# Half of a head's feature product moved ahead of the head before's attention product, with W2's splits, evictions and sums moved beside it

## Chip, cores and metric

One Trainium2 chip, one of its cores. The metric is the device time in microseconds from the kernel's start to its end.

## What is computed

A graph attention network of two layers on 512 nodes and 16,896 edges, then a residual and a layer norm. The first layer has 8 heads of 768 features, the second one head.

```
h = (x @ W).reshape(n, H, C)
alpha_s = einsum('nhc,hc->nh', h, a_s);  alpha_d = einsum('nhc,hc->nh', h, a_d)
e = leaky_relu(alpha_s[src] + alpha_d[dst], 0.2)
e = exp(e - segment_max(e, dst)[dst])
alpha = e / (segment_sum(e, dst)[dst] + 1e-16)
out = segment_sum(h[src] * alpha, dst) + b
...
h = elu(gat_layer(x, W1, ..., 8 heads, concat))
out = gat_layer(h, W2, ..., 1 head)
x = layernorm(x + out)
```

The kernel counts the edges into a dense 512 by 512 matrix and works with dense products from then on.

## The kernel before

The program is written engine by engine: each engine has its own list of instructions, in the order in which it is written out, and the engines meet at semaphores only. For each head h of the first layer there are three big products on TensorE, each in three passes of 32-bit operands split into a high and a low part (high by high, high by low, low by high):

- **B(h, n)**, n from 0 to 7 (`half_B`): x times W1 of the head. n = 2t + c is the half c (384 columns) of the row tile t (128 nodes). 18 matmuls each.
- **C(h, c)**, c from 0 to 5 (`stage_C`): the head's finished features, 128 at a time, times the rows of W2 that belong to them, summed over all heads in PSUM banks O. TensorE does C of head h-1 while the scores of head h are made.
- **A(h, c)**, c from 0 to 5 (`stage_A`): the head's rows h times its attention weights P. 12 matmuls each.

TensorE's order in head h from 3 on is: B(h, 0) to B(h, 7), C(h-1, 0), the small transposes `sources`, C(h-1, 1), the small transposes `targets`, C(h-1, 2) to C(h-1, 5) with the softmax `denominators` inside the last, A(h, 0) to A(h, 5). B, the small products and A take turns in two PSUM banks, R[0] and R[1]; the table `RING` says in which order, and `take` waits until the use two places back was released (`released`): a B by the eviction of its half, `den` by the reciprocal, an A by its scaling.

The other engines feed this. ScalarE casts the high parts of W1 and W2 out of a ring of five raw tiles Wr (`high_w1`, `high_w2`), evicts B to h32 (`evict_B`), casts h (`high_h`), and does its share of the `scores`: for each of four row tiles an Identity (L452), an Exp (L455) and the high part of P (L460). Then `high_sums` (L470) casts the column sums for the denominators. VectorE makes the sums of h with the attention vectors (`sums_h`, L717, two for a tile), in the scores the leaky maximum (L782, one input in PSUM), the product with the counts (L788, both inputs in SBUF), sums of two tiles (L793) and of all (L908), then the reciprocal of the denominators (`reciprocals`, L807), the scaling of A and the ELU. `products_W2` (L736, two for a tile) multiplies raw W2 rows of head 7 with the second layer's attention vectors; `V_OF` puts three tiles into each of two heads. GpSimd subtracts the low parts: of W1 (`low_w1`, L1060), of W2 (`low_w2`, L1066) and of P (`low_P`, L1070). SyncE issues all loads in the order of `LOADS`, each when the tile five places back has been used up.

Of the kernel before, what the change touches and what calls it, by code (L numbers as in the profile page):

```python
# [5 lines left out]
def gat_resnorm_kernel(nc, x, xT, src, dst, W1, as1, ad1, b1c, W2, as2, ad2, b2, out):  # L6
# [18 lines left out]
    EARLY = 3  # L25
# [26 lines left out]
    RING += [("r2", 2, 0), ("r1", 2, 0), ("den", 2, 0)] + [("A", 2, c) for c in range(FT)]  # L52
# [13 lines left out]
    with ctx:  # L66
# [188 lines left out]
        def sync_program(e):  # L255
# [79 lines left out]
            for h in range(EARLY, H):  # L335
                if h + 1 < H:
                    load_abc(h + 1 if h + 2 < H else H)
                for k in range(FT):
                    load_raw("w2", h - 1, k)
                if h + 2 == H:  # L340
                    load_abc(H - 1)
                if h + 1 < H:
                    for k in range(FT):
                        load_raw("w1", h + 1, k)
                for k in V_OF.get(h, ()):
# [18 lines left out]
        def scalar_program(e):  # L364
# [175 lines left out]
            for h in range(H):  # L540
# [18 lines left out]
                if h == 2:  # L559
                    high_w2(1, 4)  # L560
                    scaled_as(2, 24)
                    scores(2, 2, 0, NT, ring_bank("r2", 2, 0), (gl_value(1, FT - 1), (s_g, 2 * FT)), 8, lambda u: high_w2(1, 5) if u == 3 else None)
                    high_h(2, 0)
                    high_h(2, 1)
                    high_sums(2)
                    high_h(2, 2)
                    high_h(2, 3)
                if 0 < h < EARLY:
                    e.wait_ge(s_den, h + 1)
                    e.copy(rb[:, :], ring_bank("den", h, 0)[:, :]).then_inc(s_dc, 1)  # L570
                if h == 2:

                    e.wait_ge(s_hl, 3 * NT)
                    for k in range(3, FT):
                        high_w1(3, k)
# [864 lines left out]
```

## Time and profile before

| | us |
|---|---|
| median of 3 runs | 641.19 (640.8 to 641.33) |
| the profiled execution, its own time | 641.08 |
| its span, first to last instruction | 639.3 |
| TensorE busy | 632.1 (99% of the span) |
| VectorE busy | 518.9 (81%) |
| ScalarE busy | 337.8 (53%) |
| GpSimd busy | 204.4 (32%) |

The sum of a prediction is made against 641.08; the median of the runs is 0.11 us above it. The shares are means over stages that differ: the edge counting (the first fifth), eight heads, and the second layer from about 586 us on. The granted clock of TensorE was 0.998 in the mean.

### The profile page before, as it was taken

The page shows a single profiled execution, that of the slowest core. Times are in us where ns is not written, and L with a number is a line of the kernel's source. Part 1 is how long each engine was busy: PE and PEld are TensorE (multiplying, and loading weights), DVE is VectorE, ACT ScalarE, POOL GpSimd, SP SyncE. Part 2 cuts the span into 40 slices and gives each one's busy share as a digit, 9 for nine tenths or more (in the row PEclk, how much of TensorE's full clock was granted, in tenths as well). Part 3 has the DMA queues.
Part 4 walks back from the last instruction along what each step waited for, and adds up shares of the span by engine and source line. Part 5 has one row for each costly group of instructions (what it writes and reads, how often), then busy time and mean ns, then how long its engine had stood idle before and what let it go on. Part 6 is the DMA issues. An engine that isn't in the chain of part 4 may idle for free.

```text
span 639.3 us, 9306 instructions
## 1 busy us (share of the span) xinstructions
PE 632.1 (99%) x3426; PEld 542.7 (85%) x3426; DVE 518.9 (81%) x928; ACT 337.8 (53%) x570; POOL 204.4 (32%) x122
## 2 busy tenths in 40 slices
PE   9999999999999999999999999999999999999996
PEld 6766568989888889988898889988998899887885
DVE  8999997889989987475855685567898589889876
ACT  7899992546524754353545454463545444534382
POOL 1000000140743630357124822374136604551230
PEclk9999999999999999999999999999999999999999
DMA  8422402115154420234113330316025401800002
GB/s 313 166 75 75 154 20 99 50 54 194 51 148 140 158 74 1 60 91 148 50 51 91 97 110 25 95 45 183 26 90 159 123 26 51 293 28 1 1 2 99
DMA packets 22173, 59.36 MB, mean 93 GB/s; under 512 B 2544, under 2 KB 2800, under 8 KB 22128
## 3 DMA queue, kind: packets, MB, share of 16 engines
q1 hardware_dynamic: 21984, 58.69, 28.6%
q8 instruction: 28, 0.46, 0.3%
q14 instruction: 17, 0.14, 0.1%
q10 hardware_dynamic: 144, 0.07, 0.0%
HBM read 54.03 MB, written 4.72 MB: 92 GB/s over the span
## 4 chain that ended last, share of the span: by engine, by line
PE 82%; DVE 16%; issue 1%; DMA 0%; ACT 0%; DVEq 0%
PE O L1238 30%; PE R L1136 8%; PE R L1133 8%; PE R L1139 8%; PE R L1205 6%; PE R L1211 6%; PE R L1208 6%; DVE ohd L679 4%; DVE ohs L683 2%; PE O L1150 2%; DVE junk L717 2%; DVE junk L736 2%; PE R L1155 1%; DVE W1l L705 1%; PE O L1205 1%
## 5 line engine op out<-in xcount | busy, mean ns | idle before, releaser
L1066 POOL TENSOR_TENSOR W2l<-Wr,W2h 128x768 fp32r<-128x768 f32 x48 | 93.3, 1953 | 207.8 <-ACT W2h L411 207.8
L1070 POOL TENSOR_TENSOR Pl<-L,Ph 128x512 fp32r<-128x512 f32 x34 | 54.0, 1599 | 166.7 <-ACT Ph L460 166.4
L1133 PE MATMUL R<-W1h,xTh 128*128 128x384 f32 x312 | 105.8, 339 | 0.0
L1139 PE MATMUL R<-W1h,xTl 128*128 128x384 f32 x312 | 104.9, 336 | 0.0
L1136 PE MATMUL R<-W1l,xTh 128*128 128x384 f32 x312 | 104.8, 336 | 0.0
L717 DVE CUSTOM_DVE_ANT_0 junk<-h,abc 128x768 bf16<-128x768 f32 x64 | 62.6, 978 | 41.8 <-ACT h L423 37.4
L1238 PE MATMUL O<-W2h,gh 128*128 128x256 f32 (+1 forms) x384 | 78.6, 339 | 0.0
L1238 PE MATMUL O<-W2h,gl 128*128 128x256 f32 (+1 forms) x384 | 77.4, 336 | 0.0
L1238 PE MATMUL O<-W2l,gh 128*128 128x256 f32 (+1 forms) x384 | 77.3, 335 | 0.0
L423 ACT COPY h<-R 128x384 f32<-128x384 f32 x62 | 29.5, 477 | 73.0 <-PE R L1139 70.9
L1060 POOL TENSOR_TENSOR W1l<-Wr,W1h 128x768 fp32r<-128x768 f32 x30 | 55.4, 1868 | 37.5 <-ACT W1h L400 37.5
L1205 PE MATMUL R<-Ph,hh 128*128 128x512 f32 x168 | 66.2, 394 | 0.0
L1211 PE MATMUL R<-Ph,hl 128*128 128x512 f32 x168 | 65.9, 392 | 0.0
L1238 PEld LDWEIGHTS O<-W2l,gh 128*128 128x128 f32 x384 | 59.0, 188 | 8.0
L1238 PEld LDWEIGHTS O<-W2h,gl 128*128 128x128 f32 x384 | 59.0, 188 | 8.0
L1208 PE MATMUL R<-Pl,hh 128*128 128x512 f32 x168 | 65.2, 388 | 0.0
L1238 PEld LDWEIGHTS O<-W2h,gh 128*128 128x128 f32 x384 | 58.1, 188 | 6.5 <-issue 0.2
L1150 PE MATMUL O<-ohd,ohs 128*128 128x512 bf16 x264 | 60.3, 382 | 0.4 <-DVE ohs L683 0.4
L1133 PEld LDWEIGHTS R<-W1h,xTh 128*128 128x128 f32 x312 | 58.7, 188 | 0.7
L1136 PEld LDWEIGHTS R<-W1l,xTh 128*128 128x128 f32 x312 | 58.7, 188 | 0.4
L1139 PEld LDWEIGHTS R<-W1h,xTl 128*128 128x128 f32 x312 | 58.6, 188 | 0.0
L411 ACT CAST W2h<-Wr 128x768 fp32r<-128x768 f32 x48 | 39.5, 833 | 29.7 <-PE O L1238 22.8
(186 smaller groups left out, 1171.5 us busy)
## 6 DMA issues: line engine op xcount, KB each, us to landing
Wr<-in_W SPq DMA_DIRECT2D x101, 384.0 KB, 3.3
abc<-in_as SPq DMA_DIRECT2D x9, 384.0 KB, 4.0
abc<-in_ad SPq DMA_DIRECT2D x9, 384.0 KB, 5.9
h_rows<-h SPq DMA_DIRECT2D x8, 384.0 KB, 2.4
hl<-h_rows SPq DMA_DIRECT2D x8, 384.0 KB, 5.9
xin<-in_xT SPq DMA_DIRECT2D x6, 256.0 KB, 6.1
xr<-in_x SPq DMA_DIRECT2D x1, 1536.0 KB, 7.5
out<-res SPq DMA_DIRECT2D x4, 384.0 KB, 2.3
```

Source lines behind the costliest of these rows:

```text
L717: e.tensor_tensor_reduce(out=junk[:, :], in0=get, in1=a_ap[:, i, :], op0=ALU.mult, op1=ALU.add, scale=1.0, scalar=0.0, accum_out=asd[:, h ...
L1060: e.tensor_tensor(W1l[:, k, :], Wr[:, n, :], W1h[:, k, :].bitcast(f32), ALU.subtract).then_inc(s_w1l, 1)
L1066: e.tensor_tensor(W2l[:, m % N2, :], Wr[:, n, :], W2h[:, m % N2, :].bitcast(f32), ALU.subtract).then_inc(s_w2l, 1)
L1070: e.tensor_tensor(Pl[:, t, d0:d1], L[:, t, d0:d1], Ph[:, t, d0:d1].bitcast(f32), ALU.subtract).then_inc(s_Pl, 1)
L1133: e.matmul(bank[:, 0:HALF], xTh[:, f, xs], hi[:, ws], start=f == 0, stop=False)
L1136: e.matmul(bank[:, 0:HALF], xTh[:, f, xs], lo[:, ws], start=False, stop=False)
L1139: m = e.matmul(bank[:, 0:HALF], xTl[:, f, xs], hi[:, ws], start=False, stop=f == FT - 1)
L1150: e.matmul(O[2 * (g % 2) + q][:, :], ohs[:, r, 128 * q:128 * q + 128], ohd[:, r, :], start=j == STARTS[g], stop=j == STARTS[g + 1] - 1).th ...
L1205: e.matmul(bank[:, :], hh[:, t, cs], Ph[:, t, :], start=t == 0, stop=False)
L1208: e.matmul(bank[:, :], hh[:, t, cs], Pl[:, t, :], start=False, stop=False)
L1211: m = e.matmul(bank[:, :], hl[:, t, cs], Ph[:, t, :], start=False, stop=t == NT - 1)
L1238: mm = e.matmul(ob, ga[:, c, 128 * t:128 * t + 128], wa[:, q, lo:hi], start=first and (hi - lo == 512 or t % 2 == 0), stop=last, skip_grou ...
```

## The change

It writes the same instructions in another order; the numbers of products, casts and subtractions stay. TensorE does B(h+1, 0) to B(h+1, 3) between C(h-1, 4) and C(h-1, 5), so ahead of A(h), for h from 2 to 6; `targets` come after C(h-1, 2). For this W1 of head h+1 is cast and subtracted earlier (the last four casts between the instructions of the scores), W2's tile 5 later, and tiles 0 to 3 of the next W2 in the same head. ScalarE evicts the four early halves after `high_sums`, and B(h+1, 4) ahead of the last cast of g. VectorE does `sums_h` of the two early row tiles ahead of `reciprocals`, and in heads 5 and 6 the three `products_W2` there too.

```diff
     for h in range(EARLY, H):
-        LOADS += [("w2", h - 1, k) for k in range(FT)]
+        LOADS += [("w2", h - 1, k) for k in range(5)]
         LOADS += [("w1", h + 1, k) for k in range(FT) if h + 1 < H]
+        LOADS += [("w2", h - 1, 5)]
...
-    for h in range(EARLY, H):
-        RING += [("B", h, n) for n in range(8)]
-        RING += [("as", h, 0), ("r2", h, 0), ("r1", h, 0), ("den", h, 0)] + [("A", h, c) for c in range(FT)]
+    RING += [("r2", 2, 0), ("r1", 2, 0)]
+    for h in range(EARLY, H + 1):
+
+        RING += [("B", h, n) for n in range(4) if h < H]
+        RING += [("den", h - 1, 0)] + [("A", h - 1, c) for c in range(FT)]
+        if h < H:
+            RING += [("B", h, n) for n in range(4, 8)] + [("as", h, 0), ("r2", h, 0), ("r1", h, 0)]
...
# ScalarE
                 if h >= EARLY:
-                    for t in range(NT):
-                        evict_B(h, t, 0)
-                        if t:
-                            high_w2(h - 1, t - 1)
-                        evict_B(h, t, 1)
-                        high_h(h, t)
+
+                    evict_B(h, 2, 1)
+                    high_h(h, 2)
+                    evict_B(h, 3, 0)
+                    evict_B(h, 3, 1)
+                    high_h(h, 3)
                     scaled_as(h, 8 * h + 8)
-                    high_w2(h - 1, NT - 1)
+                    if h + 1 < H:
+                        high_w1(h + 1, 0)
+                        high_w1(h + 1, 1)
                     high_w2(h - 1, 4)
+                    scores(h, h, 0, NT, ring_bank("r2", h, 0), (gl_value(h - 1, FT - 1), (s_g, FT * h)), 3 * h + 2,
+                           lambda u, h=h: high_w1(h + 1, 1 + u) if h + 1 < H and 1 <= u <= 4 else None)
+                    high_sums(h)
+                    if h + 1 < H:
+                        evict_B(h + 1, 0, 0)
                     high_w2(h - 1, 5)
-                    scores(h, h, 0, NT, ring_bank("r2", h, 0), (gl_value(h - 1, FT - 1), (s_g, FT * h)), 3 * h + 2)
-                    high_sums(h)
-                    for c in range(2, FT):
-                        if h + 1 < H:
-                            high_w1(h + 1, c - 2)
+                    if h + 1 < H:
+                        evict_B(h + 1, 0, 1)
+                        high_w2(h, 0)
+                        evict_B(h + 1, 1, 0)
+                        high_w2(h, 1)
+                        evict_B(h + 1, 1, 1)
+                        high_w2(h, 2)
...
                 for c in range(FT):
+                    if c == FT - 1 and 2 <= h < H - 1:
+                        high_h(h + 1, 0)
                     exp_y(h, c)
+                    if c == FT - 1 and 2 <= h < H - 1:
+                        high_h(h + 1, 1)
                     if c:
                         high_g(h, c - 1)
+                    if c == FT - 1 and 2 <= h < H - 1:
+                        evict_B(h + 1, 2, 0)
...
# VectorE
-                    for t in range(NT):
-                        if t == 0:
-                            wait_abc(h)
+                    for t in (2, 3):
                         e.wait_ge(s_h32, 8 * h + 2 * t + 2)
                         sums_h(h, t, h32[:, t % 2, :], abc[:, abc_slot(h)[0], :, :])
                         low_h(h, t)
-                        if h - 1 in V_OF and t < 3:
-                            if h == H - 2 and t == 0:
-                                wait_abc(H)
-                            products_W2(V_OF[h - 1][t], 8 * h + 2 * t + 2)
...
+                if 2 <= h < H - 1:
+
+                    wait_abc(h + 1)
+                    for t in range(2):
+                        if h in V_OF and t == 0:
+                            if h + 3 == H:
+                                wait_abc(H)
+                            products_W2(V_OF[h][0], 8 * (h + 1))
+                        e.wait_ge(s_h32, 8 * (h + 1) + 2 * t + 2)
+                        sums_h(h + 1, t, h32[:, t, :], abc[:, abc_slot(h + 1)[0], :, :])
+                        if h in V_OF and t == 0:
+                            for k in V_OF[h][1:3]:
+                                products_W2(k, 8 * (h + 1) + 2)
                 if h:
                     reciprocals(h)
...
# GpSimd
                 if h >= EARLY:
-                    for k in range(FT):
-                        low_w2(h - 1, k)
+                    if h + 1 < H:
+                        low_w1(h + 1, 0)
+                        low_w1(h + 1, 1)
+                    low_w2(h - 1, 4)
+                    if h + 1 < H:
+                        for k in range(2, FT):
+                            low_w1(h + 1, k)
                 for t in range(NT):
                     low_P(h, t, 0, N)
...
-                if EARLY <= h < H - 1:
-                    for k in range(FT):
-                        low_w1(h + 1, k)
+                if h >= 2:
+                    low_w2(h - 1, 5)
+                    if h + 1 < H:
+                        for k in range(4):
+                            low_w2(h, k)
...
# TensorE
                 if h >= EARLY:
-                    for n in range(8):
+                    for n in range(4, 8):
                         half_B(h, n // 2, n % 2, take("B", h, n))
...
                 for c in range(2 if h == 1 else 0, FT):
+                    if c == FT - 1 and 2 <= h < H - 1:
+
+                        for n in range(4):
+                            half_B(h + 1, n // 2, n % 2, take("B", h + 1, n))
...
-                    if c == (0 if h == 2 else 1) and h > 1:
+                    if c == (0 if h == 2 else 1 if h == H - 1 else 2) and h > 1:
                         targets(h, 0, NT, (None, None), 2 * h + 2)
```

The first place is ScalarE in the scores of head 3, from its second Exp to what stands behind the scores. L is a score tile, Ph the high part of P, W1h and W2h the high parts of the weights. Before:

```order
L455 ACTIVATE L<-L 128x512 [waits s_lk]
L460 CAST Ph<-L 128x512 [waits s_A,s_P]
L452 ACTIVATE L<-R,as 128x512
L455 ACTIVATE L<-L 128x512 [waits s_lk]
L460 CAST Ph<-L 128x512 [waits s_P]
L455 ACTIVATE L<-L 128x512 [waits s_lk]
L460 CAST Ph<-L 128x512 [waits s_P] x2
L470 CAST gh<-y 128x512 [waits s_C,s_sd]
L400 CAST W1h<-Wr 128x768 [waits s_wr1,s_B]
L400 CAST W1h<-Wr 128x768 [waits s_wr2,s_B]
L400 CAST W1h<-Wr 128x768 [waits s_wr3,s_B]
```

After; L405, L416, L428, L457, L460, L465 and L475 are the old L400, L411, L423, L452, L455, L460 and L470:

```order
L460 ACTIVATE L<-L 128x512 [waits s_lk]
L465 CAST Ph<-L 128x512 [waits s_A,s_P]
L405 CAST W1h<-Wr 128x768 [waits s_wr4,s_B]
L457 ACTIVATE L<-R,as 128x512
L460 ACTIVATE L<-L 128x512 [waits s_lk]
L465 CAST Ph<-L 128x512 [waits s_P]
L405 CAST W1h<-Wr 128x768 [waits s_wr0,s_B]
L460 ACTIVATE L<-L 128x512 [waits s_lk]
L465 CAST Ph<-L 128x512 [waits s_P] x2
L475 CAST gh<-y 128x512 [waits s_C,s_sd]
L428 COPY h<-R 128x384 [waits s_B,s_hl]
L416 CAST W2h<-Wr 128x768 [waits s_wr1,s_C]
```

The casts of W1 have moved from behind the cast of the sums (L470, now L475) into the scores, and the evictions of the next head's first halves stand behind that cast.

The second place is VectorE in head 5, from the sums of P to the reciprocal. Before:

```order
L793 TENSOR_TENSOR rb<-L 128x512 [waits s_P]
L908 SCALAR_TENSOR_TENSOR y<-y,rb 128x512 [waits s_sd]
L913 TENSOR_TENSOR gl<-y,gh 128x512 [waits s_dh]
L807 RECIPROCAL rb<-R 128x512 [waits s_den]
L819 TENSOR_TENSOR L<-R,rb 128x512 [waits s_rc,s_A]
L819 TENSOR_TENSOR L<-R,rb 128x512 [waits s_A]
```

After, with L741, L760, L817, L831, L932 and L937 for the old L717, L736, L793, L807, L908 and L913 (a row of L760 or L741 without an input reads out the sum of the row above it):

```order
L817 TENSOR_TENSOR rb<-L 128x512 [waits s_P]
L932 SCALAR_TENSOR_TENSOR y<-y,rb 128x512 [waits s_sd]
L937 TENSOR_TENSOR gl<-y,gh 128x512 [waits s_dh]
L760 ISA junk,va<-Wr,abc 128x768 [waits s_wr1,s_asd,s_abc1,s_abc0]
L760 ISA va 128x1
L760 ISA junk,va<-Wr,abc 128x768 [waits s_v]
L760 ISA va 128x1
L741 ISA junk,asd<-h,abc 128x768 [waits s_v,s_asd,s_h32]
L741 ISA asd 128x1
L741 ISA junk,asd<-h,abc 128x768 [waits s_asd]
L741 ISA asd 128x1
L760 ISA junk,va<-Wr,abc 128x768 [waits s_asd,s_wr2]
```

Two products (L760) and two sums (L741) now stand ahead of the reciprocal; behind the last row shown come three more products, which with it make those of two further W2 tiles, the two sums of the next row tile, and then the reciprocal: ten in all.

The third place is GpSimd from the subtractions of P of head 3 to those of head 4. Before:

```order
L1070 TENSOR_TENSOR Pl<-L,Ph 128x512 [waits s_Ph] x4
L1060 TENSOR_TENSOR W1l<-Wr,W1h 128x768 [waits s_w1h] x6
L1066 TENSOR_TENSOR W2l<-Wr,W2h 128x768 [waits s_w2h] x6
L1070 TENSOR_TENSOR Pl<-L,Ph 128x512 [waits s_Ph] x4
L1060 TENSOR_TENSOR W1l<-Wr,W1h 128x768 [waits s_w1h] x6
```

After, with L1097, L1103 and L1107 for the old L1060, L1066 and L1070:

```order
L1107 TENSOR_TENSOR Pl<-L,Ph 128x512 [waits s_Ph] x4
L1103 TENSOR_TENSOR W2l<-Wr,W2h 128x768 [waits s_w2h] x5
L1097 TENSOR_TENSOR W1l<-Wr,W1h 128x768 [waits s_w1h] x2
L1103 TENSOR_TENSOR W2l<-Wr,W2h 128x768 [waits s_w2h]
L1097 TENSOR_TENSOR W1l<-Wr,W1h 128x768 [waits s_w1h] x4
L1107 TENSOR_TENSOR Pl<-L,Ph 128x512 [waits s_Ph] x4
```

All six subtractions of W1 now stand ahead of the head's own four of P, the last four of them directly ahead. Behind those of P comes a run of five of W2: tile 5 of head h-1 and tiles 0 to 3 of head h.

## Rows read from the trace of the kernel before

**Rows 1.** waits of TensorE, 244.5 to 585.8 us: us in total, times, longest

```profile
PE R L1155 <- DVE r L772: 0.3, 1, 0.3
```

**Rows 2.** busy time in two stretches: length, PE, PEld, DVE, ACT, POOL, clock, DMA, GB/s

```profile
244.50:312.70 68.20, 68.20 (x376) 61.99 (x375) 44.14 (x69) 31.67 (x50) 28.58 (x16) 1.00 0.28 81
635.00:639.20 4.20, 0.00 (x0) 0.00 (x0) 1.12 (x4) 0.29 (x1) 0.00 (x0) 0.75 0.46 187
```

**Rows 3.** timeline of TensorE in head 3 (start us, us, engine, line, operation)

```profile
244.53 0.34 PE L1133 MATMUL R<-W1h,xTh 128*128 128x384 f32 x1
...
269.49 1.54 PE L1238 MATMUL O<-W2h,gh 128*128 128x256 f32 x8
...
273.64 0.60 PE L1155 MATMUL R<-idn,asd 128*128 128x128 f32 x4
...
278.22 1.04 PE L1155 MATMUL R<-idn,r 128*128 128x128 f32 x8
...
294.31 0.40 PE L1178 MATMUL R<-gh,oner 128*128 128x512 f32 x1
...
296.18 0.40 PE L1205 MATMUL R<-Ph,hh 128*128 128x512 f32 x1
...
298.94 0.39 PE L1205 MATMUL R<-Ph,hh 128*128 128x512 f32 x1
```

**Rows 4.** timeline of ScalarE in head 3

```profile
257.21 0.48 ACT L423 COPY h<-R 128x384 f32<-128x384 f32 x1 [1.83 <-PE R L1139]
...
279.16 1.26 ACT L452 ACTIVATE L<-R,as 128x512 f32<-128x512 f32 x2
...
281.77 0.62 ACT L455 ACTIVATE L<-L 128x512 f32<-128x512 f32 x1
282.29 0.61 ACT L460 CAST Ph<-L 128x512 fp32r<-128x512 f32 x1
...
289.77 0.62 ACT L470 CAST gh<-y 128x512 fp32r<-128x512 f32 x1 [1.80 <-DVE y L908]
290.29 3.03 ACT L400 CAST W1h<-Wr 128x768 fp32r<-128x768 f32 x4
```

**Rows 5.** timeline of VectorE in head 3

```profile
288.06 1.67 DVE L908 SCALAR_TENSOR_TENSOR y<-y,rb 128x512 f32<-128x512 f32 x1
...
294.98 3.36 DVE L807 RECIPROCAL rb<-R 128x512 f32<-128x512 f32 x1 [3.53 <-PE R L1180]
```

**Rows 6.** timeline of GpSimd in head 3

```profile
291.20 7.37 POOL L1060 TENSOR_TENSOR W1l<-Wr,W1h 128x768 fp32r<-128x768 f32 x4 [0.30 <-ACT W1h L400]
```

**Rows 7.** timeline of VectorE in the scores of head 2

```profile
216.95 3.07 DVE L788 SCALAR_TENSOR_TENSOR L<-L,CT 128x512 f32<-128x512 f32 x2
220.05 1.68 DVE L793 TENSOR_TENSOR rb<-L 128x512 f32<-128x512 f32 x1
221.76 1.68 DVE L908 SCALAR_TENSOR_TENSOR y<-y,rb 128x512 f32<-128x512 f32 x1
```

**Rows 8.** timeline of GpSimd in the same stretch

```profile
215.74 2.02 POOL L1066 TENSOR_TENSOR W2l<-Wr,W2h 128x768 fp32r<-128x768 f32 x1 [2.81 <-ACT W2h L411]
217.72 6.88 POOL L1070 TENSOR_TENSOR Pl<-L,Ph 128x512 fp32r<-128x512 f32 x4
```

**Rows 9.** timeline of VectorE in head 6

```profile
458.87 0.95 DVE L736 CUSTOM_DVE_ANT_0 junk<-Wr,abc 128x768 bf16<-128x768 f32 x1
...
466.13 2.63 DVE L736 CUSTOM_DVE_ANT_0 junk<-Wr,abc 128x768 bf16<-128x768 f32 x1
```

**Rows 10.** timeline of GpSimd in the same stretch

```profile
459.86 2.66 POOL L1066 TENSOR_TENSOR W2l<-Wr,W2h 128x768 fp32r<-128x768 f32 x1 [15.95 <-ACT W2h L411]
466.10 1.85 POOL L1066 TENSOR_TENSOR W2l<-Wr,W2h 128x768 fp32r<-128x768 f32 x1 [3.58 <-ACT W2h L411]
```

**Rows 11.** timeline of TensorE in head 7

```profile
549.40 1.55 PE L1238 MATMUL O<-W2h,gl 128*128 128x256 f32 x8
551.21 1.09 PE L1155 MATMUL R<-idn,r 128*128 128x128 f32 x8 [0.27 <-DVE r L772]
```

More of the change, by code:

```diff
@@ L335, in sync_program @@
             for h in range(EARLY, H):
-                if h + 1 < H:
-                    load_abc(h + 1 if h + 2 < H else H)
-                for k in range(FT):
+                if h + 2 < H:
+                    load_abc(h + 1)
+                for k in range(5):
                     load_raw("w2", h - 1, k)
-                if h + 2 == H:
-                    load_abc(H - 1)
                 if h + 1 < H:
@@ L344, in sync_program @@
                         load_raw("w1", h + 1, k)
+                        if k == 2 and h + 3 >= H:
+                            load_abc(H if h + 3 == H else H - 1)
+                load_raw("w2", h - 1, 5)
                 for k in V_OF.get(h, ()):
@@ L560, in scalar_program @@
                     high_w2(1, 4)
+                    high_w1(3, 3)
                     scaled_as(2, 24)
-                    scores(2, 2, 0, NT, ring_bank("r2", 2, 0), (gl_value(1, FT - 1), (s_g, 2 * FT)), 8, lambda u: high_w2(1, 5) if u == 3 else None)
+                    scores(2, 2, 0, NT, ring_bank("r2", 2, 0), (gl_value(1, FT - 1), (s_g, 2 * FT)), 8, lambda u: high_w1(3, 3 + u) if u in (1, 2) else None)
                     high_h(2, 0)
@@ L565, in scalar_program @@
                     high_sums(2)
+                    evict_B(3, 0, 0)
                     high_h(2, 2)
                     high_h(2, 3)
+                    high_w2(1, 5)
+                    evict_B(3, 0, 1)
+                    high_w2(2, 0)
+                    evict_B(3, 1, 0)
+                    high_w2(2, 1)
+                    evict_B(3, 1, 1)
+                    high_w2(2, 2)
                 if 0 < h < EARLY:
@@ L614, in scalar_program @@
                         high_w1(3, c - 2)
-                    if EARLY <= h < H - 1 and c < 2:
-                        high_w1(h + 1, 4 + c)
+                    if 2 <= h < H - 1 and c == 1:
+                        high_w2(h, 3)
                     if h == H - 1 and c == 0:
@@ L714, in sums_h @@
                         e.wait_ge(s_asd, n)
-                    if not i and h - 1 in V_OF and t in range(1, 4):
-                        e.wait_ge(s_v, 2 * V_OF[h - 1][t - 1] + 2)
+                    if not i and h - 1 in V_OF and t < 2:
+                        e.wait_ge(s_v, 2 * V_OF[h - 1][2 * t] + 2)
                     e.tensor_tensor_reduce(
@@ L730, in products_W2 @@
                 for i in range(2):
-                    if i:
-                        e.wait_ge(s_v, 2 * k + 1)
+                    if i or k % 3 == 2:
+                        e.wait_ge(s_v, 2 * k + i)
                     else:
@@ L968, in vector_program @@
                         part_sums(3)
-                    if c > 1:
+                    if c == FT - 1 and 2 <= h < H - 1:
+                        low_h(h + 1, 0)
+                    if c > 1 and not (c == FT - 1 and 2 <= h < H - 1):
                         low_g(h, c - 2)
@@ L972, in vector_program @@
                         elu(h, c - 1)
+                if 2 <= h < H - 1:
+                    low_h(h + 1, 1)
                 elu(h, FT - 1)
+                if 2 <= h < H - 1:
+                    low_g(h, FT - 3)
                 low_g(h, FT - 2)
@@ L1317, in tensor_program @@
                 for c in range(2 if h == 1 else 0, FT):
+                    if c == FT - 1 and 2 <= h < H - 1:
+                        for n in range(4):
+                            half_B(h + 1, n // 2, n % 2, take("B", h + 1, n))
                     stage_C(h - 1, c, between=(lambda h=h: denominators(h)) if c == FT - 1 else None,
```

13 lines of the change are left out of this document (2 added, 11 removed).

## Prediction

> **What bounds the kernel now.** I first read the waits of TensorE through the heads (244.5 to 585.8 us): it waits 0.3 us once [rows 1]. The windows say the same: busy 68.20 of 68.20 us in head 3, granted clock 1.00 [rows 2]. So TensorE is the bound, it is full, and an order of the same matmuls can win almost nothing there. The one other gap is in head 7: a pass of C takes 1.38 us (a third of a column, below), which should have brought `targets` to 549.40 + 1.38 = 550.78, and they stand at 551.21 [rows 11]: 0.43 us lost. What the change can win in the heads is this 0.45 us or so; what it can lose is any wait that it puts in front of a TensorE that has no slack. So I asked of every moved step when TensorE now needs it and when it is ready.
>
> **The clock of a head.** Let R be the start of `targets`, 278.22 in head 3 [rows 3]. From the same rows: a half B takes (269.49 - 244.53)/8 = 3.12 us, a column C 4.15 (269.49 to 273.64), C up to `denominators` starts 16.09 after R, which is the transposes (0.9), three columns and two passes. A(h, 0) starts at 296.18, A(h, 1) at 298.94, 2.76 later. In the new order two columns follow `targets`, so B(h+1, 0) starts at R + 0.9 + 8.3 = R + 9.2, and B(h+1, 2) is due at R + 15.4. It goes into the bank of B(h+1, 0), so it waits for that half's eviction on ScalarE, and this stands behind `high_sums`, which waits for the sum L908 on VectorE. Before, L908 ends at 288.06 + 1.67 = R + 11.5 [rows 5] and L470 starts 0.04 later [rows 4]. If it stayed so, the eviction would end at R + 12.8, in time. But something else has moved in beside it.
>
> **What VectorE and GpSimd cost each other.** GpSimd's four subtractions of W1 now fall into the scores, where before they stood behind L908 [rows 6]. Head 2 of the kernel before shows such a mix, since there GpSimd is still busy with W2 when the scores run: the four subtractions of P take 6.88 us, 1.72 each, end to end behind one of W2 [rows 8], and VectorE's steps L788, L788, L793, L908 take 3.07 for two, 1.68 and 1.68 [rows 7]. One step of VectorE ends for each step of GpSimd, some 0.55 us behind it: the third subtraction of P ends at 217.72 + 0.75 x 6.88 = 222.88, L908 at 223.44. Both inputs of these steps are in SBUF. The second products of L736 show it at 768 columns: 0.95 us alone and 2.63 beside a subtraction, which itself takes 1.85 or, started behind one of VectorE's, 2.66 [rows 9, 10]. So I count them as taking turns, and the steps with an input in PSUM (L782, L807) as free: L807 took 3.36 us beside GpSimd's run of four in head 3 [rows 5, 6].
>
> The Trainium skill has this as a rule (SBUF — State Buffer, "Who interferes with whom"): a VectorE instruction with two SBUF inputs contends with a GpSimd instruction that reads SBUF, and the later one blocks fully. By it the sum below stands; if only VectorE's fast modes contended, which the same section also lists, L736 and L788 would run free and the sum would be that of the first rival. The rows of L736 decide for the former.
>
> **Edit 1: W1's split inside the scores, and the eviction behind it (heads 3 to 6).** ScalarE's pitches are 0.58 for an Identity (the pair of 1.26 less what overlaps), 0.52 for an Exp (281.77 to 282.29), 0.51 for a cast of P, and 3.03/4, about 0.74, for a cast of W1 [rows 4]; the first Identity stands at R + 0.94. The fourth tile's cast, behind three Identities, two Exps, one cast of P and its own two predecessors, ends at R + 6.5; the fifth at R + 8.9. GpSimd needs 1.84 alone (7.37/4) [rows 6] and 2.0 beside a waiting VectorE [rows 8]. In turn from here, as ends after R: subtraction of tile 2 at 4.3, first L788 4.8; tile 3 6.4, second L788 6.95; tile 4 8.6, L793 9.15; tile 5 11.0, third L788 11.5; P's first 12.7, last L788 13.25; P's second 14.4, L793 14.95; P's third 16.1, L908 16.65. The stretch from tile 5 on is 5.65 long; head 2's from the end of its W2 at 217.76 to 223.44 is 5.68 [rows 7, 8]. Then `high_sums` (pitch 0.52) and the eviction (0.48) [rows 4]: 17.7. TensorE wanted it at 15.4: a wait of 2.3 to 2.4 us in each of four heads, **9.4 us**. W1's last low part, due at 9.2 + 5 x 0.52 + 0.17 = R + 12.0, is there at 11.0: no wait, by 1.0.
>
> Head 2 has the casts of tiles 3 to 5 only and four columns behind `targets`, so its third half is due at about R + 23.7. VectorE's last sum moved from 223.44, R + 17.5, by two more turns of about 2.1 us: eviction by about R + 22. I count it at nothing.
>
> **Edit 2: the sums of the early tiles ahead of the reciprocal (heads 3 and 4).** A(h, 1) goes into the bank of the denominators and waits for L807. Before, the denominators start at 294.31, L807 runs 294.98 to 298.34, A(3, 1) starts at 298.94: 0.6 us of slack [rows 3, 5]. Now B's four halves, with the wait above, end at R + 24.0, the denominators start at R + 26.8, A(h, 1) is due at R + 31.4. VectorE makes four sums before L807, each in turn with a subtraction of W2 (2.5 us a turn: 1.85 and about 0.82, less the overlap [rows 9, 10]). The last needs the eviction of B(h+1, 3) at R + 24.7 and ends at about 28.7; L807 ends at 32.1. Late by about 0.8, twice: **1.6 us**.
>
> **Edit 3: the same with the products of W2 (heads 5 and 6).** Ten products and sums stand there instead of four. From L913 at R + 18.4 the first ends at 19.35; the next four take turns with four subtractions of W2 (2.5 each): 29.4; the last five run alone at 1.0 each: 34.5. L807 ends at 37.9, against 31.4: late by 6.5, twice: **13 us**. Before, these six products lay between the tiles of B, where VectorE idled.
>
> **Edits that I count at nothing, with their cover.** `targets` one column later: four transposes and their wait have 4.15 us more. `high_h` and `low_h` twice, ahead of B(h+1, 4)'s eviction, which now stands ahead of the last cast of g: by the same turns it ends some 0.6 us before B(h+1, 6) wants the bank; without that cover it costs up to 1 us a head. W2's tile 5 subtracted behind P: done by about R + 21, due at R + 25. In head 7 it has no such room: the second pass of C(6, 5) comes 0.2 us behind it, bounds 0 and 0.3. The loads: the ring stays five tiles, and each is released some 8 us or more before ScalarE wants its follower, but for one: in heads 5 and 6 the next W2's tile 1 follows tile 5, released at R + 21, and is cast at about R + 25 instead of 21.5. Behind it in ScalarE's queue is the eviction of B(h+1, 3), then at R + 26: ahead of A(h, 0) at 28.6, and ahead of the sums that wait for it in edit 3.
>
> **The sum.** 641.08 + 9.4 + 1.6 + 13 - 0.45 (head 7, whose VectorE has no product left in it) = 664.6; I say **664.5 us**, against the profiled execution; the median of the runs is 0.11 lower. Bounds of each term: edit 1 from 0 (L908 as early as before) to 4 x 3.5 (one more turn lost); edits 2 and 3 from 0 to 2 x 1.5 + 2 x 8.
>
> **Rivals.** (a) The engines hide it, so not slower. If GpSimd and VectorE did not hold each other up in the new order, L908 would end at R + 12.5 to 13, the eviction by R + 14.2, ahead of 15.4, and L807 would start at R + 27 even in head 5: nothing waits, head 7 gains 0.45: 640.6. It decides at 2.6 us of lost turns in the scores. For it: the pieces alone are short, VectorE is 65% busy in head 3 [rows 2]. Against: rows 7 to 10. Chance 0.12. A further 0.03 is for a gain above 1.3 us, for which I see no room. (b) Only the eviction is late, because products and sums get in pairs between subtractions and L807 keeps up: 641.08 + 9.4 + 2 = 652.5. For it: L736 ran twice in a row at 458.87 and GpSimd's 459.86 waited [rows 9, 10]. Chance 0.15. (c) Only the products are late: 656. Chance 0.08. (d) More than the sum: W1's low parts late as well, or the clock. With TensorE idle the granted clock was 0.75 over 635.0 to 639.2 [rows 2]; if each of the two long waits let it fall to 1.2 GHz and the column behind took twice its 2.76 us, that adds 5.5: 670. The Trainium skill warns of this (TensorE: Matmul & The Clock Gate, "Why this matters for your kernels"): gaps in the matmuls bring the halved clock back. Chance 0.1, the forecast's own 0.52.
>
> **Numbers.** The forecast's own range is 658 to 668. The range for 8 in 10 reaches down over (b) and (c) and up over most of (d): 649 to 671. A measurement of this kernel tells about 0.2%, 1.3 us, from no change. Slower: all but (a), 0.85; within: 0.12; faster: 0.03.
>
> **What would show it.** Waits of TensorE on the eviction (the copy of h) of about 2.3 us in heads 3 to 6 and on the reciprocal of 0.8, 0.8, 6.5, 6.5; L788, L793 and L908 at 1.3 to 1.8 us inside the scores; sums L717 and products L736 at 2 us and more ahead of L807. Wrong would be: L908 ending by R + 14.4, or the early sums running at 0.96 each.

## The result, and the profile after

The changed kernel takes **668.43 us** (median, 667.18 to 670.17) against 641.00 for the kernel before in the same job: a ratio of 1.043, with an interval of 1.0401 to 1.0458. The profiled execution took 670.17 us, 29.1 more than that of before. The first lines of its page (span; busy time of each engine) and the granted clock in 40 slices:

```profile
span 668.4 us, 9306 instructions
PE 641.3 (96%) x3426; PEld 548.8 (82%) x3426; DVE 558.9 (84%) x928; ACT 334.9 (50%) x570; POOL 216.2 (32%) x122
PEclk9999999999999999998999899998999979999999
```

TensorE's busy time rose by 9 us for the same matmuls, VectorE's by 40 and GpSimd's by 12 for the same instructions. The clock row dips where before it did not. TensorE's waits from 244.5 to 615 us, which answer to [rows 1] (L1247 is the first pass of A, L1175 that of B, L428 the eviction, L831 the reciprocal):

```profile
PE R L1247 <- DVE rb L831: 12.4, 2, 6.2
PE R L1175 <- ACT h L428: 7.2, 4, 1.8
```

These are the two kinds of wait that the prediction names. Taken from the start of one matmul to the start of the next, less the usual distance between the two (the pitch), the four on the eviction cost 1.98, 1.96, 1.96 and 1.96 us (7.9 in all), the long ones on the reciprocal (heads 5 and 6) 6.37 each (12.7), and those of heads 3 and 4 only 0.15 and 0.13.

The scores of head 3, where R (the start of `targets`) is 282.78. TensorE, VectorE, ScalarE and GpSimd in the timeline (start, us, engine), each against [rows 3 to 6]:

```profile
282.78 1.04 PE L1197 MATMUL R<-idn,r 128*128 128x128 f32 x8
...
291.96 0.34 PE L1175 MATMUL R<-W1h,xTh 128*128 128x384 f32 x1
...
300.29 0.45 PE L1175 MATMUL R<-W1h,xTh 128*128 128x384 f32 x1 [1.81 <-ACT h L428]
```

```profile
286.12 1.19 DVE L812 SCALAR_TENSOR_TENSOR L<-L,CT 128x512 f32<-128x512 f32 x1
287.28 0.75 DVE L806 SCALAR_TENSOR_TENSOR L<-R,asd,L 128x512 f32<-128x512 f32 x1
287.95 1.63 DVE L812 SCALAR_TENSOR_TENSOR L<-L,CT 128x512 f32<-128x512 f32 x1
289.61 2.23 DVE L817 TENSOR_TENSOR y<-L 128x512 f32<-128x512 f32 x1
...
297.55 1.66 DVE L932 SCALAR_TENSOR_TENSOR y<-y,rb 128x512 f32<-128x512 f32 x1
```

```profile
299.24 0.62 ACT L475 CAST gh<-y 128x512 fp32r<-128x512 f32 x1 [2.78 <-DVE y L932]
299.77 0.47 ACT L428 COPY h<-R 128x384 f32<-128x384 f32 x1
```

```profile
284.90 8.65 POOL L1097 TENSOR_TENSOR W1l<-Wr,W1h 128x768 fp32r<-128x768 f32 x4 [5.79 <-ACT W1h L405]
```

VectorE's steps with two SBUF inputs (L812, L817, L932) take 1.2 to 2.2 us; the one with an input in PSUM (L806) stays at 0.75. L932 ends at 299.21, which is R + 16.4. The eviction ends at 300.24, R + 17.5, and TensorE starts 0.05 later. In head 5 (R is 427.40) the ten sums and products stand between 445.41 and the reciprocal; VectorE's first, second and seventh of them and the reciprocal:

```profile
445.41 0.95 DVE L760 CUSTOM_DVE_ANT_0 junk<-Wr,abc 128x768 bf16<-128x768 f32 x1
...
446.40 2.48 DVE L760 CUSTOM_DVE_ANT_0 junk<-Wr,abc 128x768 bf16<-128x768 f32 x1
...
457.59 0.96 DVE L760 CUSTOM_DVE_ANT_0 junk<-Wr,abc 128x768 bf16<-128x768 f32 x1
...
461.62 3.35 DVE L831 RECIPROCAL rb<-R 128x512 f32<-128x512 f32 x1
```

It ends at R + 37.6, where the prediction had 37.9. What the prediction's sum does not hold is the clock. Windows of the same kernel, each from a matmul that ended a wait (length; PE, PEld, DVE, ACT, POOL; clock; DMA share; GB/s):

```profile
300.29:304.75 4.46, 4.46 (x17) 4.46 (x18) 3.72 (x4) 1.80 (x3) 3.75 (x3) 0.62 0.18 67
372.76:376.34 3.58, 3.58 (x11) 3.58 (x12) 2.83 (x4) 1.80 (x3) 2.87 (x3) 0.52 0.01 1
465.03:468.78 3.75, 3.75 (x9) 2.99 (x10) 0.69 (x1) 0.72 (x1) 0.00 (x0) 0.54 0.05 21
543.69:547.38 3.69, 3.69 (x10) 2.95 (x11) 0.69 (x1) 0.72 (x1) 0.00 (x0) 0.56 0.11 41
444.90:448.14 3.24, 3.24 (x18) 3.24 (x19) 3.21 (x4) 1.79 (x3) 2.52 (x3) 1.00 0.01 3
```

Behind four of the six waits that are over 1 us the granted clock falls to the lower level (1.2 GHz), and matmuls 0.17 or 0.23 us apart stand 0.32 or 0.43 apart (a spell of halved clock, below); behind the one at 444.90, as long as that at 372.76, it does not. In the first window 16 matmuls take 4.46 us and at 3.12/18 each would take 2.77; the others hold 11 (1.91), 9 and 9 at 2.76/12 (2.07 each). Lost: 1.69 + 1.67 + 1.68 + 1.62 = **6.7 us**.

The account of the 29.1 us: eviction waits 7.9, reciprocal waits 12.7 + 0.3, halved clock 6.7, head 7 - 0.43, together 27.2. Of the 1.9 left, 1.3 are a pace of B for which the prediction has no term (experiment 7), some 0.5 the first matmuls behind the four waits that these windows do not count (two on the eviction, two on the reciprocal), 0.1 longer each, and 0.2 were there before the orders part: the last matmul that they have in common starts at 223.37 us against 223.18.

### The profile page after: what moved, and what is told of

Its sections match the earlier page's. It is cut to its first block, busy times and chain, and to the rows that moved or that the text cites. A ratio compares the mean times of both kernels' runs of the same rounds, so it can differ in the third digit from the quotient of the medians.

```text
span 668.4 us, 9306 instructions
## 1 busy us (share of the span) xinstructions
PE 641.3 (96%) x3426; PEld 548.8 (82%) x3426; DVE 558.9 (84%) x928; ACT 334.9 (50%) x570; POOL 216.2 (32%) x122
## 4 chain that ended last, share of the span: by engine, by line
PE 73%; DVE 23%; ACT 2%; issue 1%; DMA 0%; DVEq 0%; ACTq 0%
PE O L1280 24%; PE R L1175 7%; PE R L1181 7%; PE R L1178 7%; PE R L1247 6%; PE R L1253 6%; PE R L1250 6%; DVE L L812 4%; DVE ohd L703 3%; DVE junk L760 3%; PE O L1192 3%; DVE junk L741 3%; DVE ohs L707 2%; DVE y L817 1%; DVE L L806 1%
## 5 line engine op out<-in xcount | busy, mean ns | idle before, releaser
L1103 POOL TENSOR_TENSOR W2l<-Wr,W2h 128x768 fp32r<-128x768 f32 x48 | 99.0, 2077 | 149.5 <-ACT W2h L416 149.5
L1175 PE MATMUL R<-W1h,xTh 128*128 128x384 f32 x312 | 108.0, 346 | 7.2 <-ACT h L428 7.2
L1178 PE MATMUL R<-W1l,xTh 128*128 128x384 f32 x312 | 106.7, 342 | 0.0
L1181 PE MATMUL R<-W1h,xTl 128*128 128x384 f32 x312 | 106.6, 342 | 0.0
L1107 POOL TENSOR_TENSOR Pl<-L,Ph 128x512 fp32r<-128x512 f32 x34 | 55.3, 1647 | 158.1 <-ACT Ph L465 157.9
L1097 POOL TENSOR_TENSOR W1l<-Wr,W1h 128x768 fp32r<-128x768 f32 x30 | 60.7, 2036 | 121.6 <-ACT W1h L405 120.8
L741 DVE CUSTOM_DVE_ANT_0 junk<-h,abc 128x768 bf16<-128x768 f32 x64 | 79.5, 1242 | 22.5 <-ACT h L428 20.7
L1247 PE MATMUL R<-Ph,hh 128*128 128x512 f32 x168 | 67.9, 404 | 12.4 <-DVE rb L831 12.4
L1175 PEld LDWEIGHTS R<-W1h,xTh 128*128 128x128 f32 x312 | 59.6, 191 | 9.4 <-ACT h L428 8.5
L1250 PE MATMUL R<-Pl,hh 128*128 128x512 f32 x168 | 66.8, 398 | 0.0
L484 ACT ACTIVATE L<-L,b1s 128x512 f32<-128x512 f32 x32 | 23.2, 724 | 76.7 <-DVE L L843 76.7
L428 ACT COPY h<-R 128x384 f32<-128x384 f32 x62 | 29.4, 476 | 48.5 <-PE R L1181 46.6
```

Of the source, the lines that this page charges most:

```text
L741: e.tensor_tensor_reduce(out=junk[:, :], in0=get, in1=a_ap[:, i, :], op0=ALU.mult, op1=ALU.add, scale=1.0, scalar=0.0, accum_out=asd[:, h ...
L1097: e.tensor_tensor(W1l[:, k, :], Wr[:, n, :], W1h[:, k, :].bitcast(f32), ALU.subtract).then_inc(s_w1l, 1)
L1103: e.tensor_tensor(W2l[:, m % N2, :], Wr[:, n, :], W2h[:, m % N2, :].bitcast(f32), ALU.subtract).then_inc(s_w2l, 1)
L1107: e.tensor_tensor(Pl[:, t, d0:d1], L[:, t, d0:d1], Ph[:, t, d0:d1].bitcast(f32), ALU.subtract).then_inc(s_Pl, 1)
L1175: e.matmul(bank[:, 0:HALF], xTh[:, f, xs], hi[:, ws], start=f == 0, stop=False)
L1178: e.matmul(bank[:, 0:HALF], xTh[:, f, xs], lo[:, ws], start=False, stop=False)
```

## The experiments

The kernel before took 640.93 us beside experiments 1 to 7 and 641.11 beside the last one. Waits are given from start to start less the usual pitch, as above, so they are some 0.15 us longer than the "us" of a wait's row. "One run" has no interval.

**1. Is it only ScalarE's order that makes the eviction late?** The eviction of B(h+1, 0) ahead of the cast of the sums.

```diff
+                    if h + 1 < H:
+                        evict_B(h + 1, 0, 0)
                     high_sums(h)
-                    if h + 1 < H:
-                        evict_B(h + 1, 0, 0)
```

> The changed kernel with one step moved: in heads 3 to 6 ScalarE evicts B(h+1, 0) ahead of the cast of the sums (L475), not behind it. Theory (VectorE and GpSimd take turns in the scores, so the sum L932 ends 16.4 us after targets, and the eviction waits for it): the eviction now follows the last cast of P and ends at R + 14.2, ahead of the 15.4 at which B(h+1, 2) wants the bank, so the four waits of 1.96 us go. But VectorE's chain to the reciprocal starts no earlier, so in heads 5 and 6 the wait at A(h, 1) grows by the same 2 us, to 8.3 each; heads 3 and 4 lose their spells of halved clock too. About 668.4 - 7.9 + 4 - 4 = 660.5 us. Rival (the eviction is late because ScalarE's own four casts of W1 fill its time): the waits stay at some 2 us in all four heads, and the time at 668.

Measured: 668.73 us, ratio 1.0439 [1.0421, 1.0458], so no gain at all. Its waits:

```profile
PE R L1247 <- DVE rb L831: 21.5, 4, 8.6
```

The eviction is no longer waited for. TensorE now waits for the reciprocal four times, 2.32, 2.29, 8.77 and 8.77 us. VectorE shows why: L932 is where it was, and the four sums behind it (the first and the last are shown) wait out a subtraction each.

```profile
297.62 1.67 DVE L932 SCALAR_TENSOR_TENSOR y<-y,rb 128x512 f32<-128x512 f32 x1
...
301.30 2.23 DVE L741 CUSTOM_DVE_ANT_0 junk<-h,abc 128x768 bf16<-128x768 f32 x1 [0.30 <-ACT h L428]
...
308.62 2.48 DVE L741 CUSTOM_DVE_ANT_0 junk<-h,abc 128x768 bf16<-128x768 f32 x1
...
311.03 3.35 DVE L831 RECIPROCAL rb<-R 128x512 f32<-128x512 f32 x1
```

The expectation added and took away waits as if they were independent. They hang on one chain, VectorE's, and taking away the first wait hands its time to the second.

**2. How much do the products cost?** The early products of W2, six in each of heads 5 and 6, cut short.

```diff
-out=junk[:, :], in0=Wr[:, n, :], in1=a2b[:, i, :]
+out=junk[:, 0:16], in0=Wr[:, n, 0:16], in1=a2b[:, i, 0:16]
```

> The changed kernel with the six products of W2 rows with the attention vectors (L760) cut to 16 of 768 columns; so the second layer's source and target terms are wrong, all waits are kept. Theory: without the six products VectorE has four long steps ahead of the reciprocal in heads 5 and 6, as in heads 3 and 4, and the waits of 6.37 us at A(5, 1) and A(6, 1) fall to 0.1 to 1; with the two spells of halved clock that is 668.4 - 12 - 4 = 652.5 us. Rival (the reciprocal is late for another reason, the denominators or the loads): waits stay above 4 us, time above 662.

Measured: 655.9 us, one run. The two long waits fell from 6.37 to 0.13 and 1.86 us; the eviction waits stayed at 1.96 to 1.98. The long waits are those of the products. The time is 3.4 above the expected one. Waits on the reciprocal of 3.2 us are left (0.59, 0.59, 0.13 and 1.86 in heads 3 to 6) where the expectation's sum left 1.0, and that sum starts from 668.4, 1.8 below the execution whose trace it was read from. Even a product of 16 columns can wait out a subtraction: one ahead of the 1.86 us took 1.82 instead of 0.17.

```profile
522.13 1.82 DVE L760 CUSTOM_DVE_ANT_0 junk<-Wr,abc 128x16 bf16<-128x16 f32 x1
```

**3. Turns or VectorE's own time?** GpSimd starts the next W2 only when the head's features are done, so the sums and products ahead of the reciprocal meet fewer subtractions.

```diff
                     if h + 1 < H:
+                        e.wait_ge(s_g, FT * h + FT)
                         for k in range(4):
                             low_w2(h, k)
```

> The changed kernel with one wait added on GpSimd: the subtractions of tiles 0 to 3 of the next W2 start when the ELUs of the head are done, not during VectorE's sums and products ahead of the reciprocal. VectorE's work stays the same. Theory (turns): in heads 5 and 6 only one subtraction is left beside the ten steps, which then run at 1.0 us each; the reciprocal ends at about R + 32 instead of R + 37.5, the waits of 6.37 us fall to about 1, and with the two spells of halved clock the time is about 668.4 - 11 - 4 = 653.5 us. Rival (ten steps are simply too much work ahead of the reciprocal, whatever GpSimd does): the waits stay at 6 us and the time at 668 or above.

Measured: 665.83 us, ratio 1.0382 [1.0365, 1.0399]. The long waits fell from 6.37 to 2.08 and 2.06, though VectorE has the same ten operations there: at least 4.3 of the 6.4 us are turns. The 2.1 left are not all VectorE's own time, since one of the ten still meets a subtraction:

```profile
449.96 2.47 DVE L760 CUSTOM_DVE_ANT_0 junk<-Wr,abc 128x768 bf16<-128x768 f32 x1
```

But the subtractions now meet the sums of the two late row tiles, which `sources` wait for:

```profile
PE R L1198 <- DVE asd L741: 8.3, 5, 1.7
PE R L1176 <- ACT h L428: 7.2, 4, 1.8
PE R L1248 <- DVE rb L831: 3.8, 2, 1.9
```

One of VectorE's two slow sums ahead of the wait at 422.19:

```profile
414.17 2.58 DVE L741 CUSTOM_DVE_ANT_0 junk<-h,abc 128x768 bf16<-128x768 f32 x1
```

So a wait was cured in one place and bought in another. The expectation had the first half only: it is 12 us short, 9.0 of them the five new waits.

**4. GpSimd's subtractions or ScalarE's casts?** The four subtractions of W1 inside the scores cut short, ScalarE's casts left as they are.

```diff
-                            low_w1(h + 1, k)
+                            low_w1(h + 1, k, 16)
```

> The changed kernel with GpSimd's subtractions of W1's tiles 2 to 5, those that fall into the scores, cut to 16 of 768 columns (the low parts are wrong, so is the output); ScalarE's casts all stay. Theory (turns): L812, L817 and L932 run at 0.7 us until P's subtractions start, L932 ends at about R + 13 instead of R + 16.4, the four waits of 1.96 us on the eviction go, and VectorE comes to the reciprocal some 3 us earlier, for a TensorE that wants it 2 us earlier: the waits in heads 5 and 6 shrink to about 5. About 668.4 - 8 - 2 - 4 = 654 us. Rival (ScalarE's casts make it late, VectorE and GpSimd do not matter): L932 stays at R + 16, the waits at 2 us, the time at 668.

Measured: 659.71 us, one run, and no eviction wait. VectorE in head 3, with R at 282.76:

```profile
286.10 0.68 DVE L812 SCALAR_TENSOR_TENSOR L<-L,CT 128x512 f32<-128x512 f32 x1
...
288.65 0.69 DVE L817 TENSOR_TENSOR y<-L 128x512 f32<-128x512 f32 x1
...
295.17 1.67 DVE L932 SCALAR_TENSOR_TENSOR y<-y,rb 128x512 f32<-128x512 f32 x1
```

The product and the sum shown run at 0.68 instead of 1.19 and 2.23, with ScalarE's four casts still between its own: the casts are not the cause. L932 ends at R + 14.1 instead of 16.4 and the eviction is in time. The long waits stay at 6.06 and 6.05, since the products are untouched. Behind each the clock is halved, longest behind the second:

```profile
532.26:538.26 6.00, 6.00 (x15) 4.70 (x16) 1.17 (x2) 0.72 (x1) 0.00 (x0) 0.52 0.03 12
```

One less the granted clock, times 6 us, is 2.9 us lost; the same working gives 1.9 behind the first (0.53 over 4 us). The time is 5.7 above the expected one. The expectation took 2 us off the long waits and 4 off the halved clock; 0.6 and 1.9 came off, and it started from 668.4, 1.8 below the execution with the trace.

**5. The same without leaving work out.** ScalarE's casts of W1 tiles 1 to 4 and GpSimd's subtractions go ahead of the scores.

```diff
                     if h + 1 < H:
                         high_w1(h + 1, 0)
-                        high_w1(h + 1, 1)
                     high_w2(h - 1, 4)
+                    if h + 1 < H:
+                        for k in range(1, 5):
+                            high_w1(h + 1, k)
```

> The changed kernel with the split of the next head's W1 moved out of the scores (nothing left out): ScalarE casts tiles 0 to 4 right behind the head's own sums, before targets, and tile 5 behind the first Identity; GpSimd in the same order. So at most two subtractions reach into the scores. Theory: as with the shortened subtractions of W1: no wait on the eviction in heads 3 to 6, waits of about 6 us left at A(5, 1) and A(6, 1) with a spell of halved clock each: 640.7 + 12 + 4 = 657 us. Rival (the raw tiles are not there so early, since each waits for a tile used up five places before): ScalarE waits on loads, the scores start late, and waits of 1 us and more appear at B(h+1, 0): 662 or more.

Measured: 659.25 us, one run. There is no eviction wait, the long ones are 4.42 each, and 1.8 us is newly waited for twice at `targets` (for the last r of the softmax preparation). The expectation, 2.3 lower, had long waits of 6 us with a spell of halved clock each; it did not have the waits at `targets`. That it comes so near is in part luck, since 3.2 us too much in one place stand against 3.6 missing in another. The spell behind the second long wait costs (1 - 0.55) x 5 = 2.3 us:

```profile
532.27:537.27 5.00, 5.00 (x13) 3.94 (x14) 0.69 (x1) 0.72 (x1) 0.00 (x0) 0.55 0.08 30
```

**6. Both cures together, and then one more.** To experiment 5 is added that GpSimd starts the next W2 when the early sums are done, which is when the reciprocal starts; and then that the third W2 tile's products stand behind the head's ELUs.

```diff
                     if h + 1 < H:
+                        e.wait_ge(s_asd, 8 * (h + 1) + 4)
                         for k in range(4):
                             low_w2(h, k)
```

> W1's split ahead of the scores as in the run before it here, and GpSimd starts W2's tiles 0 to 3 only when VectorE's sums of the two early row tiles are done, so during the reciprocal, whose input is in PSUM. Theory (turns): no wait on the eviction; the ten steps ahead of the reciprocal run at 1.0 us with one subtraction beside them, the reciprocal comes about 2.3 us late in heads 5 and 6, in time in 3 and 4, and W2's subtractions are over before the next head's sums, so the 1.8 us at sources of the run with the later W2 do not appear: 640.7 + 4.6 = 645.3, with one or two spells of halved clock up to 648 us. Rival (the subtractions now collide with the ELUs of A): waits at A(h, 2) to A(h, 5) or at B(h+1, 6), 650 or more.

```diff
-                            for k in V_OF[h][1:3]:
-                                products_W2(k, 8 * (h + 1) + 2)
+                            products_W2(V_OF[h][1], 8 * (h + 1) + 2)
...
                 low_g(h, FT - 1)
+                if h in V_OF:
+                    products_W2(V_OF[h][2], 8 * (h + 1) + 4)
```

> The run before it here, and in heads 5 and 6 the last of the three W2 tiles is multiplied behind the head's ELUs instead of ahead of the reciprocal: eight steps of 1.0 us are left there. Theory: the reciprocal is late by 0.3 us or less, TensorE waits nowhere in heads 3 to 6, and head 7 has only one product pair: 640.7 to 641.5 us, so the order of the change costs nothing once VectorE and GpSimd do not meet, and gains nothing that can be measured over before. Rival: the sums of tile 2 come 2 us later and sources wait again, 1 to 2 us in heads 6 and 7: 644 us.

Measured: 645.58 us (1.0053 [1.0035, 1.0071]) and 643.98 (1.0048 [1.0036, 1.0061]). In the traces of both no wait is left on the eviction or the reciprocal: 22.9 and 24.5 of the 27.4 us are back, by moving only the splits of W1 and W2 and one product. What is left are waits of 1.8 us at `targets`, three in the first and two in the second. So the first one's expected 645.3 was met by luck: its 4.6 us on the reciprocal did not come, and 5.4 at `targets` did. The second is 2.5 above the expected range and at the figure of its rival, but the waits are not at `sources`, where the rival has them. The five executions of the first lie between 642.12 and 647.6, and its trace is that of the slowest. VectorE (the first and the last of four steps) and GpSimd ahead of the one at 420.96 of the second kernel:

```profile
413.67 1.86 DVE L792 TENSOR_TENSOR zm<-amx,asd 128x4 f32<-128x4 f32 x1
...
419.07 1.84 DVE L798 SCALAR_TENSOR_TENSOR r<-asd,mc 128x4 f32<-128x4 f32 x1
```

```profile
413.65 7.24 POOL L1100 TENSOR_TENSOR W1l<-Wr,W1h 128x768 fp32r<-128x768 f32 x4
```

Four steps over four columns each wait out one whole subtraction of 1.8 us.

**7. The clock by itself, in the kernel before.** Its order is kept; extra reciprocals of the denominators (a half, one, one and a half, two) stand ahead of the reciprocal in heads 3 to 6, so that TensorE is made to wait for four lengths.

```diff
+                for i, w in enumerate({3: (N // 2,), 4: (N,), 5: (N, N // 2), 6: (N, N)}.get(h, ())):
...
+                    e.reciprocal(rb[:, 0:w], ring_bank("den", h, 0)[:, 0:w]).then_inc(s_pad, 1)
```

> The kernel BEFORE with added waits of TensorE of known length, to price the clock by itself: VectorE repeats the reciprocal of the denominators (same result) in heads 3 to 6: half of it, one, one and a half, two. Slack was 0.6 us, so TensorE should wait at A(h, 1) for about 1.2, 2.8, 4.6 and 6.2 us, 14.8 in sum. Theory of the clock (a wait of TensorE above some length is followed by a spell at 1.2 GHz that costs about 2 us more): the two long waits have it and the first has not, so 641.1 + 14.8 + 4 to 6 = 660 to 662 us, granted clock about 0.99. Rival (the halved clock in the changed kernel came from something else than the waits, such as the mix of products): no spell, clock 0.998, 656 us.

Measured: 662.17 us, one run, with waits of 1.24, 2.84, 4.64 and 6.24 us, 15.0 in all, and 21 us more time. Windows of 4 us behind the four:

```profile
300.60:304.60 4.00, 3.96 (x17) 3.30 (x18) 1.59 (x3) 1.62 (x3) 1.66 (x1) 1.00 0.38 147
372.20:376.20 4.00, 3.97 (x10) 3.13 (x11) 0.69 (x1) 1.45 (x2) 1.67 (x1) 0.57 0.04 15
446.70:450.70 4.00, 4.00 (x11) 3.16 (x12) 0.69 (x1) 1.44 (x2) 1.70 (x1) 0.59 0.04 16
522.80:526.80 4.00, 4.00 (x11) 3.19 (x12) 0.69 (x1) 1.44 (x2) 1.71 (x1) 0.61 0.00 0
```

Behind the last three the clock falls to the lower level for most of the 4 us. One less the granted clock, times 4 us, gives 1.7, 1.6 and 1.6 us lost: in this run the price of a spell does not grow with the wait. It is no fixed price either, as the 2.3 and 2.9 us of experiments 5 and 4 show behind waits of 4.42 and 6.05; what decides it was not tried. From the start of each of the two middle waits to the start of the next, the kernel takes 1.70 and 1.72 us more than a head of 68.14 and the wait. So the halved clock needs no more than the wait: this kernel has the old order, and nothing else of the change. The expectation had the four waits and the time (660 to 662), but a halved clock behind two of them only.

From the start of the first wait to the start of the second it is 0.60 us more, at full clock. Most of that, 0.49, is B's pace. TensorE from B(4, 0) to the C behind B's last half, and the same of head 5:

```profile
314.49 0.34 PE L1141 MATMUL R<-W1h,xTh 128*128 128x384 f32 x1
...
339.94 0.63 PE L1246 MATMUL O<-W2h,gh 128*128 128x256 f32 x3
...
387.66 0.34 PE L1141 MATMUL R<-W1h,xTh 128*128 128x384 f32 x1
...
412.62 0.62 PE L1246 MATMUL O<-W2h,gh 128*128 128x256 f32 x3
```

Eight halves take 25.45 us the first time, 3.18 each, and 24.96 the second, 3.12 each, with the same instructions. In the changed kernel 21 halves of heads 3 to 7 take 3.18, among them all early ones ahead of a wait: 21 x 0.06 = 1.3 us.

**8. The last wait removed.** To experiment 6's second kernel: GpSimd subtracts W1 tiles 1 to 5 when the four small steps are done.

```diff
                     if h + 1 < H:
+                        e.wait_ge(s_r12, 2 * h + 2)
                         for k in range(1, FT):
```

> The run before it here (one product later) with one wait added on GpSimd: the subtractions of W1's tiles 1 to 5 start when VectorE's four short steps behind the maxima (zm, mc, and the two r, 128x4 each) are done. In that run each of the four, 0.16 us alone, stood 1.8 us beside a subtraction, and targets were 1.8 us late in heads 5 and 6 (and 1.8 more in other runs of the order). Theory: the four take 0.7 us again, targets are in time in every head, the subtractions run some 3 us later and one more of them reaches into the scores, the eviction (due at R + 15.4) stays in time by about 1 us. No wait of TensorE in heads 3 to 7: 640.6 us, against 641.0 before, a ratio of 0.999 to 1.000. Rival (the room that was left is used up): a wait on the eviction of 1 us or less per head, 642 to 645 us.

Measured: **641.92 us** (11 runs) against 641.11 (15 runs), 1.0013 [1.0004, 1.0022]. The first and the last of the four small steps, and GpSimd behind them:

```profile
414.00 0.16 DVE L792 TENSOR_TENSOR zm<-amx,asd 128x4 f32<-128x4 f32 x1
...
414.47 0.15 DVE L798 SCALAR_TENSOR_TENSOR r<-asd,mc 128x4 f32<-128x4 f32 x1
```

```profile
414.70 9.09 POOL L1100 TENSOR_TENSOR W1l<-Wr,W1h 128x768 fp32r<-128x768 f32 x5 [0.68 <-DVE r L798]
```

TensorE waits nowhere from 244.5 to 615 us, and still this kernel takes 0.8 us more than the one before. The reason is in the same trace: a head takes 68.37 us instead of 68.14. The early halves of head 6 and the late ones, each from the first matmul to the C behind them:

```profile
428.70 0.34 PE L1179 MATMUL R<-W1h,xTh 128*128 128x384 f32 x1
...
441.42 0.40 PE L1284 MATMUL O<-W2h,gh 128*128 128x256 f32 x2
...
462.53 0.34 PE L1179 MATMUL R<-W1h,xTh 128*128 128x384 f32 x1
...
475.01 0.39 PE L1284 MATMUL O<-W2h,gh 128*128 128x256 f32 x2
```

12.72 against 12.48: 3.18 and 3.12 each. Five heads with four such halves are 20 x 0.06 = 1.2 us, less the 0.43 of head 7 is 0.8, which is what was measured. The expectation had the gain and not the pace.

## Why the prediction was right

**Direction and size.** 664.5 was forecast, 668.43 measured: inside 649 to 671, and 0.4 above the forecast's own 658 to 668. The waits came in the forecast's places, on the forecast's releasers. Against the profiled execution the sum is 5.6 low (664.6 and 670.17): it lacks 6.7 us of halved clock, 1.3 of B's pace and 0.7 of small things, and holds 3.1 too much in edits 1, 2 and 3. That these partly cancel is luck, and the terms tell more than the total.

**"What VectorE and GpSimd cost each other".** Shown by experiments 4 and 8, in which the same VectorE steps run at 0.68 and 0.16 once GpSimd is short or elsewhere, and by L806 and L831, which have an input in PSUM and never slowed (0.75 and 3.35 us in every trace; in the first kernel of experiment 6 the same reciprocal took 3.36 us at 309.88, beside GpSimd's run that began at 309.20). The Trainium skill's rule (SBUF — State Buffer, "Who interferes with whom"), that VectorE with two SBUF inputs and GpSimd reading SBUF lock each other out for a whole instruction, agrees with these traces, down to the 0.16 us step that took 1.86.

**Edit 1, 9.4 us forecast, 7.9 measured.** Mechanism right; the eviction ended at R + 17.5 instead of 17.7, and B(h+1, 2) was due at R + 15.5, not 15.4. Two small errors of one sign, four times. A slip in the working, of no weight: by its own pitches the eviction would have ended at R + 12.55, not 12.8, had L908 stayed where it was, so the turns had 2.9 us to lose and not rival (a)'s 2.6.

**Edit 2, 1.6 forecast, 0.3 measured.** The term was mis-sized because the clock fell in between: after the eviction wait of head 3 TensorE ran slowly, came to A(h, 1) at R + 32.9 instead of 31.4, and found the reciprocal nearly done. Experiment 2 bears this out: its heads 3 and 4 have the same order and the same eviction waits but no halved clock, and the reciprocal is waited for 0.59 us in each, against the forecast's 0.8. Experiment 1 shows the other side: without the eviction wait the same sums cost 2.3 us a head. Edits 1 and 2 are one delay on VectorE's chain that TensorE meets at whichever place comes first, so their terms do not stand or fall one by one.

**Edit 3, 13 forecast, 12.7 measured.** Experiments 2 and 3: the products' place is the cause, and at least two thirds of each wait are turns.

**Head 7, 0.45 forecast, 0.43 measured.**

**What the sum lacked.** The clock. Rival (d) had it with a chance of 0.1, priced at 5.5 us for the two long waits; it came at 6.7 us for those two and two of the eviction waits, beside a forecast that was otherwise right. It should have been a term and not a rival: the row with clock 0.75 [rows 2] was at hand, and experiment 7 shows the fall behind every wait of 2.84 us and more. The Trainium skill's warning (TensorE: Matmul & The Clock Gate, "Why this matters for your kernels") that gaps in the matmuls bring the halved clock back agrees with these traces behind every wait of 2.84 us and more; behind waits near 2 us they show it some of the time only. Rivals (b) and (c) each had only one kind of wait, and both kinds came; rival (a) fell as the kernel stood, but experiment 8 shows its premise to be sound: where the engines do not hold each other up, TensorE's new order waits nowhere.

## What to carry to other kernels

Before moving a GpSimd operation, list the VectorE steps that will stand beside it and have two inputs in SBUF: each can cost one whole GpSimd operation, however small it is (128x4 steps of 0.16 us took 1.8 here). When several engines' waits hang on one late chain, moving the first waiter can just hand the delay to the next (experiment 1); shorten the chain. On a TensorE without slack, count for a wait of 3 us or more another 1.6 to 2.9 us of halved clock behind it, as these runs had, and leave room for it behind one of 2 us.

## What was not expected of the hardware

- Waits of nearly one length end differently: behind 1.96 us (372.76) the clock was halved, behind 1.96 us (444.90) and behind 2.32 and 2.29 (experiment 1) it was not; in experiment 3 it was behind 2.08 and not behind 2.06. From 2.84 us on it always was (11 waits in five kernels). What decides in between was not tried. It goes with the spread of the changed kernel's four executions: 667.18 and 667.49 us at a mean granted clock of 0.989 and 0.988, 669.37 and 670.17 at 0.984 and 0.983.
- B's half of 18 matmuls has two paces at full clock, 3.12 and 3.18 us, each kept until TensorE waits or turns to another product. The old order shows both (experiment 7), and so does the new one: in the second kernel of experiment 6 the four early halves of head 6 take 3.18 each and those of heads 4, 5 and 7 take 3.12 to 3.14. So the order alone does not decide it. Its cause stays open; it is worth 0.24 us a head here, and is all that the last kernel still loses.
